# Two experts per token for the first 2560 tokens, all eight for the rest, with rows scattered and added by GpSimd

## The reference

```python
x = x + _L0_gnn_ref(_layernorm(x), ...)        # softmax(leaky_relu(f1 + f2^T) + mask) @ layernorm(x)
x = x + _L0_ffn_ref(_layernorm(x)[None], ...)[0]

logits = xf @ gate_w + gate_b                  # 8 logits a token
probs = softmax(logits); top2_vals, top2_idx = top_k(probs, 2)
cw = zeros((N, 8)).at[arange(N)[:, None], top2_idx].add(top2_vals)
for w1, bb1, w2, bb2, we in experts:           # W1 128 x 256, W2 256 x 128
    h = gelu(xf @ w1 + bb1)
    acc = acc + we[:, None] * (h @ w2 + bb2)
```

## Time and profile before

| | us |
|---|---|
| runs | 510.32, 510.36, 511.88 (median 510.36) |
| span of the profiled execution, which is its time in all that follows | 509.6 |
| attention stage, up to the first expert matmul | 320.0 |
| expert stage, from there | 189.6 |
| PE busy | 471.5 |
| DVE busy | 425.4 |
| ACT busy | 234.3 |
| POOL busy | 46.7 |

### The profile page before, as it was taken

The page is one execution under the profiler, slowest core; times in us unless marked ns, Lnnn a source line. Parts: engine busy times, 40 slices in busy tenths (PEclk is TensorE's granted clock), DMA queues, the critical chain, the costliest instruction groups (busy, mean ns, idle before and its releaser), DMA issues.

```text
span 509.6 us, 5787 instructions
## 1 busy us (share of the span) xinstructions
PE 471.5 (93%) x1712; PEld 221.2 (43%) x1712; DVE 425.4 (83%) x726; ACT 234.3 (46%) x362; POOL 46.7 (9%) x98
## 2 busy tenths in 40 slices
PE   2799999799979999899998999798999999999996
PEld 2773434245335444454444534343434444444442
DVE  0447679798998998989989897579899898988985
ACT  1539810113200200102001124689888888988883
POOL 8903202001010020020000000100000000000000
PEclk9859999999989999999999999999999999999999
DMA  6999999999809639389000000423443346445520
GB/s 193 183 106 105 105 106 202 168 163 90 76 2 97 66 30 105 31 77 88 0 0 0 1 0 21 153 84 82 104 82 113 124 118 122 84 103 112 126 50 22
DMA packets 35042, 44.49 MB, mean 87 GB/s; under 512 B 2592, under 2 KB 24528, under 8 KB 34768
## 3 DMA queue, kind: packets, MB, share of 16 engines
q0 software_dynamic: 17920, 18.88, 37.4%
q1 hardware_dynamic: 16288, 25.37, 19.7%
q10 hardware_dynamic: 816, 0.03, 0.1%
HBM read 92.38 MB, written 2.23 MB: 186 GB/s over the span
## 4 chain that ended last, share of the span: by engine, by line
PE 55%; DVE 23%; issue 7%; DMA 7%; ACT 6%; DVEq 1%; SPq 0%; ACTq 0%
PE bank L1044 20%; DVE c L828 11%; PE bank L1089 4%; PE bank L1091 4%; PE bank L1090 4%; DMA x<-in_x 4%; PE bank L1078 4%; PE bank L1080 4%; PE bank L1079 4%; DMA share<-in_L_gnn_inlayer 2%; DVE maskT L640 2%; PE bank L966 2%; ACT mask L567 2%; DVE xs L714 2%; DVE maskT L891 2%
## 5 line engine op out<-in xcount | busy, mean ns | idle before, releaser
L1044 PE MATMUL bank<-c,Y 128*128 128x512 f32 x512 | 232.9, 603 | 8.9 <-DVE c L828 8.3
L828 DVE SCALAR_TENSOR_TENSOR c<-g_row,r_col,maskT 128x512 f32<-128x512 f32 (+1 forms) x256 | 182.1, 744 | 17.8 <-PE bank L1044 14.0
L1044 PEld LDWEIGHTS bank<-c,Y 128*128 128x128 f32 x512 | 93.1, 191 | 132.7 <-issue 75.5
L885 DVE TENSOR_TENSOR mask<-mask,share 128x1024 f32<-128x1024 f32 x64 | 78.2, 1223 | 21.0 <-ACT mask L567 18.5
L567 ACT ACTIVATE mask<-bank,b1T 128x512 f32<-128x512 f32 x128 | 83.8, 688 | 22.8 <-PE bank L1080 21.2
L891 DVE TENSOR_TENSOR maskT<-mask,maskT 128x1024 f16<-128x1024 f32 x64 | 78.4, 1225 | 0.0
L574 ACT ACTIVATE maskT<-mask 128x1024 f16<-128x1024 f32 x64 | 67.4, 1053 | 3.2 <-DVE mask L885 3.1
L1089 PE MATMUL bank<-maskT,w2h 128*128 128x512 f16 x128 | 49.1, 383 | 5.7 <-DVE maskT L891 5.2
L1090 PE MATMUL bank<-maskT,w2h 128*128 128x512 f16 x128 | 49.0, 383 | 0.0
L1091 PE MATMUL bank<-maskT,w2l 128*128 128x512 f16 x128 | 49.0, 383 | 0.0
L1078 PE MATMUL bank<-share,w1h 128*128 (+1 forms) x128 | 48.5, 379 | 0.0
(11 more groups left out here) (145 smaller groups left out, 355.4 us busy)
## 6 DMA issues: line engine op xcount, KB each, us to landing
share<-shares SPq DMA_DIRECT2D x16, 1024.0 KB, 8.3
mask<-in_adj POOLq DMA_DIRECT2D x24, 512.0 KB, 17.2
mask<-in_adj POOLq DMA_DIRECT2D x32, 128.0 KB, 25.6
share<-in_L_gnn_inlayer SPq DMA_DIRECT2D x2, 1024.0 KB, 10.0
share<-in_x POOLq DMA_DIRECT2D x8, 256.0 KB, 12.2
out<-c SPq DMA_DIRECT2D x8, 256.0 KB, 3.8
share<-in_L_ffn_W SPq DMA_DIRECT2D x1, 1024.0 KB, 21.6
W_sb<-in_L_gnn_W SPq DMA_DIRECT2D x1, 64.0 KB, 2.0
```

The lines of the kernel that those rows point to most:

```text
L828: dve.scalar_tensor_tensor(c[:, k % CR].rearrange("p (s i) -> p s i", i=32), g_row[:, bass.ds(s * ST, ST)].rearrange("p (s i) -> p s i", i ...
L885: dve.tensor_tensor(hw[:, e % 2], h[:, e % 2], wb[:, e].unsqueeze(1).to_broadcast([P, FC, ST]), ALU.mult).then_inc(hw_done, 1)
L1044: mm(bank[:, par, :], Y[:, k], c[:, k % CR], start=(k == 0), stop=(k == NK - 1)).then_inc(c_used, 1)
```

## The change

The loops of the attention stage are written out. The first five supertiles (`HEAD = 5`, 2560 tokens) are routed early: their logits are complete in supertile 6, where DVE now runs the router for them, PE counts with triangular and all-one matrices how many earlier rows chose the same expert (`rank`), and DVE works out for each of the two choices of a token its slot in a list sorted by expert, in which each expert starts on a multiple of 256 rows. The list has 27 tiles of 256 rows (`NT`), and the expert of each tile is written to SBUF (`expert`).

A row is 132 words: the high and low f16 halves of the token, its number (`row_id`) and padding. The halves are made before PE's transposition now: ACT makes the high one (`post_c`), GpSimd the low one for supertiles 0 to 5 (`low_rows`), DVE for 6 and 7. PE transposes both in f16. GpSimd scatters the rows into `sorted_x` in DRAM, 128 rows with one indirect DMA: 20 for the first choices, then, after these have landed and the row numbers have been raised by N, 20 for the second. SP, which has cleared `sorted_x` before with three stores, loads tile after tile, up to twelve ahead.

For each tile PE and ACT load its expert into a register, PE turns the rows (`turn_x`), ACT copies them (`copy_x`), and after the first layer and GELU DVE makes the halves of the hidden layer (`high`, `low`). The second layer has the hidden layer as stationary operand, so that its result has tokens on partitions; DVE sums the two column blocks of the result (`evict`), and GpSimd scatters the rows unweighted to `choice_y` in DRAM by their row numbers, two indirect DMAs a tile (`place_choice`).

The last three supertiles are computed for all experts, in 24 steps after the tiles, with the second layer turned the same way and DVE adding each expert's result with its share to x2 (`add_dense`). SP loads the scattered results of the first five meanwhile, GpSimd weights and adds them, and SP stores. The second bias is a matmul of K = 2 in both parts.

```diff
+    HEAD = 5
+    GROUP = ((0, HEAD * TS), (HEAD * TS, NK))
+    NT = (2 * HEAD * ST + E * (TW - 1)) // TW
+    STEPS_D = [(s, e) for s in range(HEAD, NS) for e in range(E)]
...
@@ block.sync
+            for t in range(NT):
+                if t == 0:
+                    for s_in in sorted_in:
+                        sp.wait_ge(s_in, 16 * HEAD * TS)
+                    sp.wait_ge(turned, NS * NP)
+                if t >= XR:
+                    sp.wait_ge(y_out[(t - XR) % YR], 16 * TP * ((t - XR) // YR + 1))
+                sp.dma_start(xt[:, t % XR].rearrange("p s w -> p (s w)"),
+                             sorted_x[TW * t:TW * t + TW].rearrange("(p s) w -> p (s w)", s=TP)).then_inc(xt_in[t % XR], 16)
...
+            for s in range(HEAD):
+                for v in range(2):
+                    sp.dma_start(yin[:, s, v], choice_v[s, v]).then_inc(yin_in[s], 16)
...
@@ block.gpsimd
+            def low_rows(s):
+                pool.wait_ge(xtok_ready, s + 1)
+                pool.tensor_tensor(rows16[:, s * TS:s * TS + TS, D:2 * D], xn2[:], rows16[:, s * TS:s * TS + TS, 0:D],
+                                   ALU.subtract).then_inc(xlp_ready, 1)
+            def place_row(v, n):
+                pool.indirect_dma_start(out=sorted_x, out_offset=bass.IndirectOffsetOnAxis(ap=slot_i[:, v, n:n + 1].bitcast(U32), axis=0),
+                                        in_=rows[:, n], in_offset=None).then_inc(sorted_in[v], 16)
...
+            for s in range(4, NS):
+                low_rows(s - 4)
+                load_adj(s, s % 2)
...
+            low_rows(4)
+            low_rows(5)
+            pool.wait_ge(filled, 48)
+            pool.wait_ge(slot_ready, 1)
+            for n in range(HEAD * TS):
+                place_row(0, n)
+            second_ids()
+            for n in range(HEAD * TS):
+                place_row(1, n)
             pool.wait_ge(xs_ready, NS)
             pool.tensor_copy(x2[:, (NS - 1) * TS:NS * TS, :], xs[:]).then_inc(x2_kept, 1)
+            for t in range(NT):
+                place_choice(t)
+            for s in range(HEAD):
+                part = slice(s * TS, s * TS + TS)
+                pool.wait_ge(yin_in[s], 32)
+                for v in range(2):
+                    for i in range(TS):
+                        ins = pool.tensor_scalar(yin[:, s, v, i], yin[:, s, v, i], share[:, v, s * TS + i:s * TS + i + 1], None,
+                                                 ALU.mult)
...
@@ block.vector
+                    if s == HEAD + 1 and k == 1:
+                        route_a(0)
+                    if s == HEAD + 1 and (6 <= k < 19 or k >= 23) or last:
+                        next(routers[0], None)
...
+            for t in range(NT):
+                high(t)
+                if t >= LAG:
+                    evict(t - LAG)
+                low(t)
...
+            for j in range(ND):
+                if j > 0:
+                    low_dense(j - 1)
+                if j < LAG:
+                    evict(NT - LAG + j)
+                else:
+                    add_dense(j - LAG)
...
@@ block.tensor
+            def ffn1(t):
+                e = experts[t]
+                pe.wait_ge(xtT_ready, t + 1)
+                need(pe, gelu_done, t - 1)
+                for f in range(FC):
+                    dst = bank[:, HB[t % 2], TW * f:TW * f + TW]
+                    wh, wl = (w[:, bass.ds(e * H + P * f, P)] for w in (w1h_, w1l_))
+                    mm(dst, wh, xtT[:, t % 2, 0], start=(f == 0), stop=False)
+                    mm(dst, wh, xtT[:, t % 2, 1], start=False, stop=False)
+                    ins = mm(dst, wl, xtT[:, t % 2, 0], start=False, stop=(f == 1))
+                ins.then_inc(h_ready, 1)
...
+                for f in range(FC):
+                    w2 = w2_[:, bass.ds(e * (FC * 2 * D) + f * 2 * D, 2 * D)]
+                    w2h = w2_[:, bass.ds(e * (FC * 2 * D) + f * 2 * D, D)]
+                    for i in range(TP):
+                        mm(dst[:, i], hh[:, r, f, P * i:P * i + P], w2, start=(f == 0 and i == 0), stop=False)
+                        mm(dst[:, i, 0:D], hl[:, r, f, P * i:P * i + P], w2h, start=False, stop=False)
+                ins = mm(dst[:, :, 0:D], scale16[:], b2_[:, bass.ds(e * D, D)].unsqueeze(1).to_broadcast([2, TP, D]),
+                         start=False, stop=True)
...
+            for t in range(NT):
+                experts.append(pe.value_load(expert[0:1, t:t + 1], min_val=0, max_val=E - 1))
+                if t == 0:
+                    turn_x(0)
+                if t + 1 < NT:
+                    turn_x(t + 1)
+                ffn1(t)
+                if t >= LAG:
+                    ffn2(t - LAG)
```

More of the change, by code:

```diff
@@ L814, in _ @@
+                yield
+                dve.wait_ge(dve_step, done)
+                done = mark(dve.tensor_reduce(tile_e, past, AX_X, ALU.add))
+                yield
+                dve.wait_ge(dve_step, done)
+                dve.tensor_scalar(expert[:], tile_e, float(E - 1), None,
+                                  ALU.min).then_inc(expert_ready, 1)
             BN = (12, 13, 17, 18)
             TURNS = (15, 20, 24, 28)
-            def supertile(s, par, n, first=False, last=False):
-                router = route_b(*ROUTE[0])
+            routers = [route_b(r) for r in range(2)]
@@ L819, in supertile @@
+            def supertile(s, first=False, last=False):
+                par = s % 2
                 for k in range(NK):
@@ L845, in supertile @@
                         post_b(s - 1, BN.index(k))
-                    if not first and k == 25:
+                    if last and k == 23:
                         post_c(s - 1)
@@ L940, in _ @@
-            for st in range(PEELED):
-                experts(st)
-            with dve.Fori(PEELED, NS) as st:
-                experts(st)
-            low(NS * E - 1, E - 1)
-            add_out(NS - 1)
+            for s in range(NS):
+                supertile(s, first=(s == 0), last=(s == NS - 1))
+            post_0(NS - 1)
+            post_a(NS - 1)
+            post_sum(NS - 1)
+            post_b(NS - 1, 0)
+            dve.wait_ge(post_step, (NS - 1) * POST + 1)
+            post_b(NS - 1, 1)
@@ L1124, in _ @@
-            for st in range(PEELED):
-                experts(st)
-            with pe.Fori(PEELED, NS) as st:
-                experts(st)
-            for e in range(E - LAG, E):
-                ffn2((NS - 1) * E + e, e, NS - 1)
-            turn_y(NS - 1)
+                    dst, x = bank[:, HD[j % 2][f], :], xT_of(s)
+                    mm(dst, wh, x[:, 0], start=True, stop=False)
+                    mm(dst, wh, x[:, 1], start=False, stop=False)
+                    mm(dst, wl, x[:, 0], start=False, stop=True).then_inc(dh_ready, 1)
@@ L1133 @@
+            for j in range(ND):
+                ffn1_dense(j)
+                if j < LAG:
+                    ffn2(NT - LAG + j)
+                else:
+                    ffn2_dense(j - LAG)
+            for j in range(ND - LAG, ND):
+                ffn2_dense(j)
 _INS = ["x", "adj", "L0_gnn_inlayer2", "L0_gnn_W", "L0_gnn_b", "L0_gnn_w1", "L0_gnn_b1", "L0_gnn_w2", "L0_gnn_b2",
```

757 lines of the change are left out of this document (426 added, 331 removed).

## The result

The changed kernel took 514.63 us (median of 4; 514.22 to 514.83), the kernel before 511.12 beside it: a ratio of 1.007 [1.0046, 1.0093], slower by 3.6 us where 26 us less were forecast. The profiled execution took 514.22 us, its span 512.0.

The account below looks back on a forecast made before the run. PE and DVE were taken to bound the attention stage, PE the expert stage. First tile 337.8 + 1.3 + 1.5 + tiles 67.5 + dense 70.8 + tail 5 = 483.9, with 0.76 outside the span 484.7, forecast 485; range 455 to 515.

Parts of the forecast that it names:

- Attention stage, 318: Attention stage's end: 320 less 7.5, plus 5, plus 4 (supertile 6), less 3.7 (supertile 7); bounds 311 and 326.
- Scatter, 337.8: Before the experts: 40 indirect DMAs at 1.1 us from 286, plus 2.7 and 5.1; first tile ready at 337.8.
- middle wait: Mid-scatter: GpSimd waits for the first 20 indirect DMAs to land and updates ids, 2.7 us.
- Rival 3: Attention stage: GpSimd's subtractions and scatter descriptors stop DVE's mask products, stage ends at 326, total 493; chance 0.10.
- Sorted tiles, 70.3 with cold start and first copy: Expert stage: 27 tiles at 2.5 us on PE, 67.5, plus 1.3 half-clock start and 1.5 first turning and copying.
- rival 2: Sorted tiles: register addresses cost nothing extra, DVE sets the pace at 1.9 us a tile, total 469; chance 0.11.
- price of register addresses: Sorted tiles on PE: 15 of 19 instructions carry sequencer-computed addresses, 0.125 us each, within 2.1 us a tile.
- Dense part and tail, 75.8: Last three supertiles: 24 steps at PE's 2.95 us, 70.8 (bounds 70 and 93), plus 5 for the tail.
- Outside the span: Whole run: 0.76 us added to the span of 483.9 to give the median, 484.7.
- Rival 4: Scatter: indirect DMAs cost more; each 0.1 us adds 4 us, from 1.74 us the gain is gone; chance 0.12.
- The cover named for GpSimd's results and sums: Expert stage: GpSimd's 2.2 us a tile hides below PE's 2.5, its later 40 us behind 71 us of dense steps.
- signs of being wrong: Profile: 40 pieces over 1.7 us, tiles over 3 us, small dense matmuls 0.1 us apart, or GpSimd finishing last.

Follow-up runs that it names:

- e7: Changed kernel with its 40 indirect scatter transfers made plain ones to fixed blocks, sorting left out: 480.03 us, 0.9417 of the kernel before.
- e6: Changed kernel with sorted tile t taking expert t mod 8, fixed at build, no register loads or addresses: 512.39 us, 1.0041 of the kernel before.
- e3: Changed kernel with supertile 7's post work and the second routing moved ahead of the first sorted tile: 506.82 us, 0.9918 of the kernel before.
- e5: Changed kernel plus 150 dummy matmuls on PE after supertile 7, keeping it busy during the scatter: 512.32 us, 1.0045 of the kernel before.
- e2: Changed kernel with a third buffer for the hidden rows of a dense step: 507.11 us, 0.9946 of the kernel before.
- e8: Changed kernel with 2048 sorted tokens, third hidden-row buffer and PE's supertile 7 sums before the first sorted tile: 486.33 us, 0.9508 of the kernel before.
- e9: Changed kernel with third hidden-row buffer and supertile 7's chain ahead of the sorted tiles, still 2560 sorted tokens: 504.52 us, 0.9871 of the kernel before.
- e18: Changed kernel with the three one-partition VectorE instructions that find the tiles' experts placed 12 products later: 510.23 us, 1.0 of the kernel before.

## Why the prediction was wrong

Its sum, 483.9, against the span of 512.0:

- **Attention stage, 318: right.** From one copy of the attention result (L611, before L481) to the next, supertile 6 grew by 3.2 us and supertile 7 shrank by 4.3, for 4 and 3.7. The first supertile ended 2.0 us later, which no term has. The small terms were not tested one by one.
- **Scatter, 337.8: measured 351.55, +13.75. Failed.** The 40 transfers took 59.25 us, not 44: 6.5 for the hold, and 8.7 because a transfer comes every 1.27 to 1.4 us. Its busy time of 1.0 was close to my 1.1, but busy time isn't the distance to the next one; the plain issues of the earlier trace rows, mean 0.660, say nothing of the gap that e7 shows to be absent for plain ones and the trace to be 0.30 for indirect ones. Start (+0.8), middle wait (2.0 for 2.7) and end (3.5 for 5.1) give back 1.5. Rival 3 had the right two engines (GpSimd's reading and VectorE's two-input work) but looked for the loss in the products; 6.5 us came with one small comparison that I had counted among 25 router instructions.
- **Sorted tiles, 70.3 with cold start and first copy: measured 65.6 (351.55 to 417.17), -4.7, by two errors that met.** A later tile took 1.94 us (389.15 to 416.33 for 14), nearly rival 2's 1.9, though PE sets it (busy for 29.48 of 30.00 us from 390 on) and not VectorE (27.55). The price of register addresses from the earlier trace rows, 0.125 a matmul, doesn't carry over (e6: at most 0.09 us a whole tile). About 27 x 0.56 = 15 us were gained. Some 10 were lost in the first twelve tiles, because supertile 7's chain stands between them, which I had not costed at all (e3); the clock's share is not told apart from nothing (e5). That the two errors met is luck.
- **Dense part and tail, 75.8: measured 94.8, +19.0. Failed.** I compared each engine's sum with PE's (2.95 against 2.5 and 2.3) and took the largest. With two buffers the three pieces on two engines form a circle of 3.55; 24 x 0.63 = 15.2 us. e2 shows it, and that even the open step is 3.17; the hand-overs that a bound by busy time leaves out are my reading of that, untested. The rest, 3.8, is lead-in and tail.
- **Outside the span** 2.2 us, not 0.76. The 0.76 set the median of some runs against the span of another; each run of the kernel before lies 1.6 to 1.7 above its own span, each of the changed kernel 2.0 to 2.2.

Sum: 483.9 + 13.75 - 4.7 + 19.0 = 511.95, plus 2.2. Rival 4 named the right place and half the mechanism, but its price, 1.74 us a transfer, was not reached; with the dense circle beside it, 61 us of scatter were enough. That e8 came out near the forecast, at 486.33, confirms no term of it: it sorts 2048 tokens and has two of the mends.

The cover named for GpSimd's results and sums, PE's 2.5 us a tile and the 71 us of dense steps, held only because both parts were slow: in e3 the tiles wait for GpSimd's results, and in e2 and e9 the end waits for its drain, which the sum had put at nothing.

Of the signs of being wrong that the prediction named none showed: the 40 pieces took 1.19 us on average, later tiles 1.94, small dense matmuls started 0.055 apart, and GpSimd ended before VectorE. The first three ask for the price of one piece; the loss lay in the gaps and waits between pieces.

## What to carry to other kernels

Price a transfer by the distance between two starts, not by its busy time, and where a phase has nothing beside it, ask first whether less of it could be hidden altogether: one supertile of the five moved back to the dense way was worth more than any repair of the hole. Where pieces of a step alternate between two engines, follow the buffer round the circle before taking the busiest engine as the limit. A mended stretch hands the end to the next engine, here GpSimd, whose program closes 8.1 us after its last addition, so mends are added up only after a run of both.

## What the runs showed of the hardware

- Behind a VectorE comparison with two inputs on one partition of 128, the next GpSimd instruction that reads SBUF took 7.5 to 8.1 us (2.21 in e18), in most runs until VectorE stood still; with the comparison and the two instructions behind it on 128 partitions it took 1.10. A memset on GpSimd was not held.
- GpSimd issues indirect transfers of 128 rows of 528 B every 1.27 us beside an idle VectorE (0.97 busy, 0.30 between), plain ones of the same rows every 0.55, beside a busy VectorE.
- The drain that closes GpSimd's program ended 8.1 us after its last addition in e2, e9 and the changed kernel; in e2 and e9 that set the end of the execution, 3.6 and 3.7 us after SP was through with the last store.
- Matmuls whose weights are addressed from a register ran 0.11 us apart for 256 columns, half of the 0.215 that 512 columns take without one.
